# One stationary block of values and ones, block turns on VectorE, and shifted scores begun by halves of the heads

## The reference

```python
xn = layernorm(x)
Q, K, V = xn @ Wq.T + bq, ctx @ Wk.T + bk, ctx @ Wv.T + bv      # split into 16 heads of 16
attn = softmax(Q @ K.T / 4, axis=-1)                            # per head
x = x + concat_heads(attn @ V) @ Wo.T + bo
x = x + ffn(layernorm(x))          # each token through the expert with the highest router score
```

## Time and profile before

| | |
|---|---|
| median of the runs | 344.95 us |
| profiled execution, time / span | 344.3 us / 342.4 us |
| TensorE busy | 324.2 us (95%) |
| VectorE / ScalarE / GpSimd busy | 156.1 / 139.0 / 155.5 us (46 / 41 / 45%) |
| mean granted TensorE clock | 0.994 |
| attention stage | about 160 us, then the expert tiles |

### The profile page before, as it was taken

The page is one execution under the profiler, slowest core; times in us unless marked ns, Lnnn a source line. Parts: engine busy times, 40 slices in busy tenths (PEclk is TensorE's granted clock), DMA queues, the critical chain, the costliest instruction groups (busy, mean ns, idle before and its releaser), DMA issues. The chain is left out here.

```text
span 342.4 us, 9262 instructions
## 1 busy us (share of the span) xinstructions
PE 324.2 (95%) x3317; PEld 280.9 (82%) x3317; DVE 156.1 (46%) x350; ACT 139.0 (41%) x433; POOL 155.5 (45%) x400
## 2 busy tenths in 40 slices
PE   7899999999999999988999899999999999999990
PEld 6677877787778777766888899999999999999990
DVE  2657778777777778998272111111121111111200
ACT  2555555555555555435431333223332223332220
POOL 5786666666666674667236622223322221111121
PEclk9999999999999999999999999999999999999997
DMA  5991444454400000173239766655456674445100
GB/s 168 322 348 47 155 155 155 156 155 155 156 34 33 33 33 33 32 260 116 70 119 351 234 243 176 250 200 186 172 186 192 198 213 174 150 146 197 59 2 0
DMA packets 28700, 51.90 MB, mean 152 GB/s; under 512 B 3117, under 2 KB 18607, under 8 KB 28528
## 3 DMA queue, kind: packets, MB, share of 16 engines
q1 hardware_dynamic: 24720, 43.00, 36.6%
q0 software_dynamic: 2944, 8.13, 8.7%
q10 hardware_dynamic: 992, 0.17, 0.3%
HBM read 45.01 MB, written 7.21 MB: 152 GB/s over the span
## 5 line engine op out<-in xcount | busy, mean ns | idle before, releaser
L520 ACT ACTIVATE hT<-bank,b_sb 128x128 f32<-128x128 f32 x184 | 52.4, 368 | 108.7 <-PE bank L1096 107.7
L1096 PE MATMUL bank<-xeT,w_slot 128*128 128x128 f32 x736 | 86.9, 275 | 1.5 <-issue 1.2
L1096 PEld LDWEIGHTS bank<-xeT,w_slot 128*128 128x128 f32 x736 | 85.8, 192 | 3.0 <-issue 2.0
L1111 PE MATMUL bank<-w_sb,hT 128*128 x368 | 83.0, 379 | 0.4 <-ACT hT L520 0.4
L1111 PEld LDWEIGHTS bank<-w_sb,hT 128*128 128x128 f32 x368 | 68.3, 190 | 9.1 <-issue 0.6
L392 POOL DMA_INDIRECT out<-y_sb,scatter_i x23 | 23.1, 1006 | 107.7 <-DVE y_sb L825 101.6
L631 DVE TENSOR_REDUCE peaks<-bank 128x4 f32<-128x512 f32 x64 | 39.7, 684 | 0.7 <-PE bank L867 0.7
L810 DVE COPY xeT<-bank 128x256 f32<-128x256 f32 x20 | 8.5, 424 | 66.4 <-PE bank L1082 66.4
L485 ACT ACTIVATE probsT<-bank 128x512 f32<-128x512 f32 x64 | 33.0, 603 | 10.9 <-PE bank L955 10.9
L825 DVE TENSOR_TENSOR y_sb<-gathered,bank 128x256 f32<-128x256 f32 x23 | 9.7, 421 | 52.8 <-PE bank L1111 52.8
L464 ACT ACTIVATE k_pair<-bank,bk_pair,own 128x128 f32<-128x128 f32 x64 | 24.0, 456 | 14.8 <-PE bank L916 14.8
(11 more groups left out here) (154 smaller groups left out, 417.7 us busy)
## 6 DMA issues: line engine op xcount, KB each, us to landing
w_slot<-in_w SPq DMA_DIRECT2D x23, 1024.0 KB, 5.4
w_sb<-in_w SPq DMA_DIRECT2D x8, 1024.0 KB, 6.0
records<-record SPq DMA_DIRECT2D x16, 256.0 KB, 2.3
gathered<-in_x SPq DMA_DIRECT2D x3, 512.0 KB, 7.8
gathered<-in_ctxT SPq DMA_DIRECT2D x3, 512.0 KB, 7.5
b_sb<-in_b SPq DMA_DIRECT2D x1, 1024.0 KB, 10.4
gathered<-records,gather_i POOLq DMA_INDIRECT x23, 4.5
out<-y_sb,scatter_i POOLq DMA_INDIRECT x23, 2.4
```

The lines of the kernel that those rows point to most:

```text
L520: ins = a.activation(hT[:, s % 2, c], H_BANK[s % 2][c // 4][:, P * (c % 4):P * (c % 4 + 1)], ACT.Gelu, bias=b1_sb[:, bass.ds(e * FC + c, 1)])
L1096: ins = t.matmul(H_BANK[s % 2][f // 4][:, P * (f % 4):P * (f % 4 + 1)], w1_slot[:, s % 2, c, P * f:P * (f + 1)], xeT[:, s % 2, c], start=( ...
L1111: ins = t.matmul(Y_BANK[s % 2][:, 0:D], hT[:, s % 2, c], w2_flat[:, bass.ds(e * (FC * D) + c * D, D)], start=(c == 0), stop=(c == FC - 1))
```

## The change

The stationary block of `weigh_values` becomes 16 value columns of a head and 16 columns of ones (`v_ones`), so one matmul gives 16 rows of weighed values and 16 rows of the sum of the weights. The 16 matmuls no longer accumulate in pairs: each writes a block of 32 partitions with four pieces of 32 columns, and the 16 blocks fill U_BANK. `sum_probs` and its block of ones go. VectorE's `weigh` now turns the whole bank in blocks of 32 x 32 (queries then lie on partitions, heads along the columns), takes the reciprocal of one sum for each head, multiplies, and turns the product back into `oT`. In `shifted_scores` the loop over the heads of the pairs is now outside, and its first half waits only for the first of the two instructions of `shift_queries` (`q2_half`). ScalarE's copy of the values is one instruction of 256 columns and not two of 128.

```diff
@@ -93,16 +93,17 @@
         top = sb("top", [P, PAIR])
         own_top = sb("own_top", [P, PAIR])
         bk_pair = sb("bk_pair", [P, PAIR, KC])
-        ones_pair = sb("ones_pair", [P, PAIR, STRIP])
         xn = sb("xn", [P, 2, D])
         xnT = sb("xnT", [P, KC, P])
         q_whole = sb("q_whole", [P, 2, KC, P])
         k_pair = sb("k_pair", [P, 2, KC, PAIR, P])
         q_pair = sb("q_pair", [P, 2, PAIR, KC, P])
-        v_pair = sb("v_pair", [P, 2, KC, STRIPS, PAIR * PAIR, HD])
+        v_ones = sb("v_ones", [P, 2, HEADS, 2, HD])
         peaks = sb("peaks", [P, KC, P])
         probsT = sb("probsT", [P, STRIPS, KC * PAIR, P])
-        recips = sb("recips", [P, D])
+        turned = sb("turned", [P, HEADS, 2, HD])
+        recips = sb("recips", [P, HEADS])
+        weighed = sb("weighed", [P, HEADS, HD])
         oT = sb("oT", [P, KC, P])
         record = sb("record", [P, RECORDS, 2 * D])
         x2T = sb("x2T", [P, KC, P])
@@ -160,7 +161,7 @@
 
         names = """consts_pool masks_done wq_in wk_in wv_in wo_in wr_in bias_in w2_in b2_in bv_in bk_in bq_in
             bv_rep_done bv_ready bo_done ln1_stats ln1_aggr ln1_root xn_done xb_done xT_ready xT_taken q_ready q_taken qa_done
-            k_ready k_taken v_ready v_taken s_ready max_done nm_ready q2_done st_ready exp_done av_ready recip_done o_done
+            k_ready k_taken v_ready v_taken s_ready max_done nm_ready q2_half q2_done st_ready exp_done av_ready turned_done recip_done weighed_done o_done
             y_ready x1_done ln2_stats ln2_aggr ln2_root xn2_done x2T_ready x2T_taken logits_ready logits_taken
             onehot_done rank_ready rank_taken places_done place_hot_dve place_hot_pool chosen_done table
             table_pool rank_saved tiles_done codes_done slots_coded ids_ready ids_taken gather_ready scatter_ready slots_done
@@ -263,8 +264,7 @@
 
             def attention_constants():
                 g.memset(peaks[:], 0.0)
-                g.memset(v_pair[:], 0.0)
-                g.memset(ones_pair[:], 0.0)
+                g.memset(v_ones[:], 1.0)
                 g.memset(before[:], 1.0)
                 g.memset(ones[:], 1.0)
                 g.memset(onehot[:], 0.0)
@@ -274,9 +274,6 @@
 
             def routing_constants():
                 pool.wait_ge(sm["consts_pool"], 3)
-                for i in range(PAIR):
-                    g.memset(ones_pair[:, i, HD * (PAIR - 1 - i):HD * (PAIR - i)], 1.0)
-
                 g.affine_select(out=before[:], in_=before[:], compare_op=ALU.is_ge, fill=0.0, base=-1,
                                 pattern=[[1, P]], channel_multiplier=-1)
                 g.iota(iota_i[:], pattern=[[1, P]], base=0, channel_multiplier=0)
@@ -468,9 +465,7 @@
             def take_v(b):
                 act.wait_ge(sm["v_ready"], b + 1)
                 wait_for(act, "av_ready", b - 1)
-                strips = v_pair[:, b % 2].rearrange("p c j m d -> p (c j) m d")
-                for i in range(PAIR):
-                    ins = a.copy(strips[:, :, PAIR - i], V_BANK[:, 0:D].rearrange("p (r e d) -> p r e d", e=PAIR, d=HD)[:, :, i])
+                ins = a.copy(v_ones[:, b % 2, :, 0], V_BANK[:, 0:D].rearrange("p (h d) -> p h d", d=HD))
                 ins.then_inc(sm["v_taken"], 1)
 
             def take_xT(b):
@@ -638,14 +633,21 @@
                     mine = q_pair[:, b % 2, i].rearrange("p c s -> p (c s)")
                     ins = v.scalar_tensor_tensor(out=mine, in0=M_BANK[:, 0:D], scalar=top[:, i:i + 1], in1=mine,
                                                  op0=ALU.mult, op1=ALU.add)
+                    if i == 0:
+                        ins.then_inc(sm["q2_half"], 1)
                 ins.then_inc(sm["q2_done"], 1)
 
             def weigh(b):
                 dve.wait_ge(sm["av_ready"], b + 1)
-                v.reciprocal(recips[:], U_BANK[:, D:2 * D]).then_inc(sm["recip_done"], 1)
+                v.transpose(turned[:].rearrange("p h m d -> p (h m d)"), U_BANK[:]).then_inc(sm["turned_done"], 1)
+                dve.wait_ge(sm["turned_done"], b + 1)
+                v.reciprocal(recips[:], turned[:, :, 1, 0]).then_inc(sm["recip_done"], 1)
                 dve.wait_ge(sm["recip_done"], b + 1)
+                v.tensor_tensor(weighed[:], turned[:, :, 0], recips[:].unsqueeze(2).broadcast_to([P, HEADS, HD]), ALU.mult)\
+                    .then_inc(sm["weighed_done"], 1)
+                dve.wait_ge(sm["weighed_done"], b + 1)
                 wait_for(dve, "y_ready", b)
-                v.tensor_tensor(oT[:].rearrange("p c s -> p (c s)"), U_BANK[:, 0:D], recips[:], ALU.mult)\
+                v.transpose(oT[:].rearrange("p c s -> p (c s)"), weighed[:].rearrange("p h d -> p (h d)"))\
                     .then_inc(sm["o_done"], 1)
 
             def residual(b):
@@ -868,13 +870,6 @@
                                        k_pair[rows, b % 2, c].rearrange("p i k -> p (i k)"), start=True, stop=True)
                 ins.then_inc(sm["s_ready"], 1)
 
-            def sum_probs():
-                for i in range(PAIR):
-                    for j in range(STRIPS):
-                        ins = t.matmul(U_BANK[STRIP * j:STRIP * (j + 1), D:2 * D], ones_pair[:, i],
-                                       probsT[:, j, i::PAIR], start=(i == 0), stop=(i == PAIR - 1))
-                return ins
-
             def keep_busy(turns):
                 for _ in range(turns):
                     t.transpose(K_BANK[:, 0:P], ident[:], ident[:])
@@ -889,10 +884,11 @@
                 for c in range(KC):
                     for i in range(PAIR):
                         for j in range(STRIPS):
-                            two = v_pair[:, b % 2, c, j, PAIR * i:PAIR * (i + 1)].rearrange("p m d -> p (m d)")
-                            t.matmul(U_BANK[STRIP * j:STRIP * (j + 1), P * c:P * (c + 1)], two, probsT[:, j, PAIR * c + i],
-                                     start=(i == 0), stop=(i == PAIR - 1))
-                sum_probs().then_inc(sm["av_ready"], 1)
+                            both = U_BANK[STRIP * j:STRIP * (j + 1), 2 * P * c:2 * P * (c + 1)]
+                            ins = t.matmul(both.rearrange("p (t i s) -> p t i s", i=PAIR, s=STRIP)[:, :, PAIR - 1 - i],
+                                           v_ones[:, b % 2, PAIR * (STRIPS * c + j + 1) - 1 - i].rearrange("p m d -> p (m d)"),
+                                           probsT[:, j, PAIR * c + i], start=True, stop=True)
+                ins.then_inc(sm["av_ready"], 1)
 
             def route(b):
                 pe.wait_ge(sm["x2T_taken"], b + 1)
@@ -946,9 +942,9 @@
                 ins.then_inc(sm["xT_ready"], 1)
 
             def shifted_scores(b):
-                pe.wait_ge(sm["q2_done"], b + 1)
-                for c in range(KC):
-                    for i in range(PAIR):
+                for i in range(PAIR):
+                    pe.wait_ge(sm["q2_half" if i == 0 else "q2_done"], b + 1)
+                    for c in range(KC):
                         for j in range(STRIPS):
                             rows = slice(STRIP * j, STRIP * (j + 1))
                             h = PAIR * c + i

```

## The result

The changed kernel takes 336.58 us (median of four runs, 336.01 to 337.17) against 345.06 before: a ratio of 0.9756, 95% interval 0.9731 to 0.9781, so 8.5 us less. The forecast was 334.2, inside a range of 332.6 to 340.0. The direction and the loop were right; about a fifth of the gain is missing, and the forecast's own range, 332.6 to 336.0, was missed by 0.6 us.

What follows compares the result with a forecast made beforehand. TensorE (busy 95%) bounds a 9.24 us loop. Savings of 1.28 + 0.29 + 7.20 + 0.73 + 0.33 + 1.00 = 10.8 us give 334.2 us beside the median, range 332.6 to 340.0 (own range to 336.0).

Steps and rivals of the forecast that it cites:

- the loop: Each 9.24 us turn: maxima, turn_peaks, project_v, shifted_scores, project_q, transposes, project_o beside the exps, scores, residual, next maxima.
- the 2.54 us: Time from the start of the maxima to turn_peaks without sum_probs; it was 3.07 us, so 0.53 comes off a turn.
- the wait that moves to `peaks`: Ahead of turn_peaks TensorE would wait for VectorE's maxima: 0.56 us of the 1.09 of sum_probs becomes this wait.
- the 0.19 us of the early start: Genuine wait at shifted_scores, gone each turn: it comes 1.27 us after turn_peaks and not 1.46.
- The turns on VectorE: In weigh, turns of 512 and 256 columns run at the plain rate: 0.68 and 0.42 us.
- weigh_values in pieces: Writing four pieces leaves its TensorE slot at 0.79 us; rival of double cost: 345.4 us, chance 0.05.
- The slower rivals: Turns at half rate, 338.8 us, chance 0.10; pieces, 345.4, 0.05; weigh becomes the bound, 359 to 380, 0.09.
- the product is 0.42 by its own row: In weigh, the product of 256 columns was taken at 0.42 us of the 1.87 us sum.
- the limit of 2.32: Up to 2.32 us weigh is hidden behind project_q and the transposes; above that project_o waits in each turn.
- 0.45 in hand: Room left to weigh, at 1.87 us, before project_o would have to wait.
- the 2.59 which the count of instructions alone gave: Weigh by the number of instructions alone: two more cost 0.39 us, from 2.20 to 2.59.
- the early start does nothing: Rival at shifted_scores: an extra wait or project_v holding TensorE longer loses 12 x 0.19 = 2.3 us; 336.5, chance 0.12.

Runs made afterwards that it cites:

- add_bo first: The changed kernel with GpSimd's add_bo ahead of own_queries in all turns but 14: 335.1 us, ratio 0.9720; again on another chip 334.28, 0.9697.
- the late start: The changed kernel with shifted_scores as before, one wait for both shifts: 336.69 us, ratio 0.9764; the same with add_bo ahead of own_queries: 337.13, 0.9776.
- the control: The kernel before, with GpSimd's add_bo ahead of own_queries: 344.9 us against 345.02, ratio 0.9994.
- half of sum_probs: The kernel before with 4 of the 8 matmuls of sum_probs, so its output is not the reference's: 339.82 us, ratio 0.9846.

## Why the prediction was right, and where it was not

The loop, the 2.54 us and the wait that moves to `peaks` held, and so did the 0.19 us of the early start where weigh leaves room (0.18 in the kernel before, 0.17 with add_bo first). The turns on VectorE, which no row showed, took 0.70 and 0.45 us (forecast 0.68 and 0.42), the reciprocal 0.25 (0.26). The Trainium skill ("Vector Engine (DVE) Microarchitecture Reference", 3.8 The reshape front-end and per-opcode configuration) gives one element per cycle and lane. The trace agrees with it, read as the rate of a plain copy: the two turns differ by 0.25 us for 256 columns, 1.0 ns a column, and the forecast took 1.02. weigh_values in pieces takes 0.81 us of loads, as before. The slower rivals have no part.

The step that failed is one term: "the product is 0.42 by its own row". That row was of a product out of PSUM. The new one reads two tensors in SBUF and takes 1.00 us beside add_bo. So weigh was 2.51 and not 1.87, over the limit of 2.32, and the "0.45 in hand" was not there. With a product of 0.42 weigh takes 1.93 (with add_bo first, in turn 6, from 66.89 to 68.82), so the sum of its links was sound but for this; that 2.51 lies near the 2.59 which the count of instructions alone gave is chance. TensorE paid 0.16 us a turn: 2.59 and not 2.43 to project_o. Moving add_bo gave it back, 8.48 us a turn, which is the forecast's 8.52 and a little. From the maxima of turn 1 to those of turn 13 the two profiles take 104.6 and 102.3 us. In time it is 1.2 to 2.3 us by the ratios (0.9756 and 0.9765 against 0.9720 and 0.9697, not measured side by side on one chip), out of 2.4 missing.

The measured time is that of a rival, "the early start does nothing" (336.5), and as a statement on the changed kernel that is right: with the late start it takes 336.69. But neither of the rival's reasons holds. There is no extra wait, and project_v holds TensorE no longer than was read; the 0.17 us come on TensorE and are lost again behind the product. That the wide range holds is partly luck: it was drawn to take in the rivals, not this.

The trace before had the sign, on the other engine. Timelines of VectorE and GpSimd in turn 14:

```profile
147.40 0.81 DVE L712 TENSOR_TENSOR gathered<-iota_row,place 128x640 f16<-128x640 f32 x1
```
```profile
147.35 0.19 POOL L357 TENSOR_TENSOR slot_sum<-fold 128x3 f32<-128x3 f32 x1
147.62 0.65 POOL L380 TENSOR_TENSOR slot_code<-slot_sum,slot_f 128x3 f32<-128x3 f32 x1
```

An addition of three columns took 0.65 us where its neighbour took 0.19, and ended at 148.27, beside a VectorE instruction of two SBUF tensors that ended at 148.21. The Trainium skill ("SBUF — State Buffer", SBUF: two separate sides) has the rule: a VectorE instruction with two SBUF inputs and a GpSimd instruction that reads SBUF take turns at a shared pair of ports, whichever starts first keeping it to its end. The rows agree with it: a product that began beside a GpSimd instruction waited for its end (1.00, 0.80 and 0.65 us), GpSimd waited in turn 14 of the trace before, and shift_queries in the control, with one input in PSUM, did not. They show one thing besides: the held product ends 0.26 to 0.29 us after GpSimd's instruction, not the 0.42 that it takes alone.

Smaller misses, from the profiles. sum_probs was worth 0.87 us and not 1.09 where TensorE is the bound: in turn 1 turn_peaks came 3.03 us after the maxima and not 3.90. The last loads of weigh_values are now followed by 0.20 us of idle (83.21), which was not there ahead of sum_probs; why it stands there was not tried. So the new wait at turn_peaks is about 0.34 us and not 0.56, of which its row shows 0.25 as idle. In turn 12 the choice of experts follows weigh on VectorE, and the residual follows that, so the whole of the longer product counts (9.07 us, not 8.65): with a product of 1.00 us in it the turn took 9.07, and in the three profiles with add_bo first, where that product took 0.42, 0.44 and 0.67, it took 8.49, 8.52 and 8.74. From the shift of turn 13 to the comparison the forecast had 0.33 us from a shorter weigh; the count of tiles did come 0.30 earlier, but GpSimd lost it again beside VectorE:

```profile
138.98 1.17 POOL L325 TENSOR_SCALAR q_pair<-q_whole,own_top 128x256 f32<-128x256 f32 x2
...
140.43 0.71 POOL L352 TENSOR_TENSOR fold<-passed_gap 128x12 f32<-128x12 f32 x1
```

They took 0.93 and 0.21 before. That these two are the same contention is read from the overlap and was not tried apart.

## What to carry to other kernels

Price a moved operation by where its operands lie, not by its shape: the product went from 0.42 to 1.00 us when its first input moved from PSUM to SBUF and GpSimd's addition was running at that moment. When two engines' chains feed each other once a turn, such a meeting can lock in and become the length of the turn; then the cheapest cure is another order on the engine that has time. And a wait taken away on the bounding engine is worth only as much as the next engine in the loop is early: of 1.09 us, 0.53.

## What was not expected of the hardware

TensorE's granted clock fell to half in two profiles, those of the two variants of the changed kernel with the late start. TensorE had idled 1.4 us ahead of turn_peaks(15), where sum_probs no longer fills the time. Stretches of the changed kernel with the late start (length, busy us of PE, PEld, DVE, ACT, POOL, then granted clock, DMA):

```profile
143.00:146.00 3.00, 1.66 (x28) 1.38 (x21) 2.47 (x5) 0.17 (x1) 2.04 (x3) 0.95 0.39 124
146.00:148.00 2.00, 2.00 (x25) 1.67 (x27) 1.93 (x5) 0.00 (x0) 1.59 (x4) 0.50 0.71 201
148.00:150.00 2.00, 2.00 (x27) 1.73 (x20) 0.57 (x2) 1.01 (x3) 1.54 (x6) 0.72 0.58 160
```

0.50 is the lower of the two levels, 1.2 GHz. The 16 shifted scores there took 1.80 us of loads and not 0.98. The same idle stretch in the profile of the changed kernel, 1.44 us, was followed by 1.00, so the idle time alone does not decide it.

Something like it stands at the start of the changed kernel's first profile. TensorE idled 1.10 us ahead of turn 0, and twice eight loads of 0.97 us then took 1.83 and 1.73, until past 10 us; this is 0.9 of the 1.3 us at its start. The profile with half of sum_probs has the same behind 0.95 us of idle. But the granted clock of these stretches reads 1.00, so that the clock is the cause is not shown. In other profiles 1.06 and 1.22 us of idle at this place were followed by loads of 0.97.
